# The shifted layers of a transformer stack on one Trainium2 core: the value products in rows of 32, and the products of a tile ordered by array shape

## The reference, cut to what matters

```
x' = shift_tokens(x)                      # second half of the features from the token before
q, k, v = split(x' @ Wqkv)                # 16 heads of 64
q, k = rotary(l2norm(q) * qs), rotary(l2norm(k) * ks)
for each window of 32 tokens: keys of the window before and of its own (64), masked
    out = softmax(8 * q k^T) v
x = x + out @ Wo
x = x + (a * gelu(gate)) @ W2 + b2,  a, gate = split(layernorm(shift_tokens(x)) @ W1 + b1)
```

## Time and profile before

| | |
|---|---|
| median of three runs | 4652.31 us (4650.04 to 4658.37) |
| profiled execution, own time | 4656.79 us |
| its span | 4655.0 us |
| TensorE busy (matmul) | 4112.3 us, 88% |
| VectorE busy | 3561.9 us, 77% |
| ScalarE busy | 2988.6 us, 64% |
| GpSimd busy | 2212.4 us, 48% |
| granted TensorE clock, mean | 0.935 |
| the same, 400 to 3700 us | 1.00 |

### The profile page before, as it was taken

One profiled execution on the slowest core, in us unless ns is written; L12 is line 12 of the kernel. 1 busy time (PEld: TensorE's weight loads), 2 busy tenths in 40 slices (PEclk: granted clock), 3 DMA queues, 4 the chain that ended last, 5 costly groups with the idle time before them and its releaser, 6 DMA issues. The chain is left out here.

```text
span 4655.0 us, 112822 instructions
## 1 busy us (share of the span) xinstructions
PE 4112.3 (88%) x40172; PEld 2362.1 (51%) x40175; DVE 3561.9 (77%) x8496; ACT 2988.6 (64%) x5496; POOL 2212.4 (48%) x1392
## 2 busy tenths in 40 slices
PE   8969999999999999999999999999999953747635
PEld 5644555555555555555555555555555532635533
DVE  7878888888888888888888888888888846356441
ACT  3427777777777777777777777777777745645302
POOL 0006665665656656566566656656565500140006
PEclk9989999999999999999999999999999975868557
DMA  1013222322223222232222322223222200000202
GB/s 41 1 54 67 62 58 62 80 59 61 60 60 81 63 59 60 58 82 65 59 59 60 76 65 63 57 64 75 64 60 61 58 17 12 1 1 6 82 9 35
DMA packets 187828, 246.44 MB, mean 53 GB/s; under 512 B 88677, under 2 KB 129383, under 8 KB 187367
## 3 DMA queue, kind: packets, MB, share of 16 engines
q1 hardware_dynamic: 182054, 240.47, 22.2%
q0 software_dynamic: 5632, 4.33, 0.7%
HBM read 41.65 MB, written 14.30 MB: 12 GB/s over the span
## 5 line engine op out<-in xcount | busy, mean ns | idle before, releaser
L1234 POOL TENSOR_TENSOR f_rot_a<-f_rot_a,f_norm 128x1024 f32<-128x1024 f32 x384 | 730.4, 1902 | 996.1 <-DVE f_norm L1073 963.6
L1226 POOL TENSOR_TENSOR f_rot_a<-f_rot_a,f_rot_b 128x1024 f32<-128x1024 f32 x384 | 908.5, 2366 | 246.3 <-issue 213.6
L832 PE MATMUL f_bank<-f_w_vo,f_xs_t 128*64 128x512 f32 x3072 | 828.5, 617 | 24.5 <-ACT f_vo L1303 24.5
L1303 ACT ACTIVATE f_vo<-f_bank 128x512 f32<-128x512 f32 x768 | 457.0, 595 | 395.9 <-PE f_bank L832 385.9
L1294 ACT ACTIVATE f_squares<-f_bank 128x512 f32<-128x512 f32 x768 | 456.4, 594 | 295.5 <-PE f_bank L819 215.6
L1052 DVE TENSOR_TENSOR f_rot_a<-f_bank,f_rot 128x512 f32<-128x512 f32 x768 | 525.0, 684 | 83.4 <-DVE f_stat L1101 42.3
L1055 DVE TENSOR_TENSOR f_rot_b<-f_bank,f_rot 128x512 f32<-128x512 f32 x768 | 516.8, 673 | 0.0
L864 PEld LDWEIGHTS f_bank<-f_k_t,f_q_t 128*32 128x32 f32 x12288 | 313.6, 109 | 315.4 <-issue 162.4
L1059 DVE TENSOR_REDUCE f_sums<-f_squares 128x16 f32<-128x1024 f32 x384 | 464.9, 1211 | 1.6
L1315 ACT ACTIVATE f_k_t<-f_bank 64x512 f32<-64x512 f32 x768 | 449.2, 585 | 4.8 <-PE f_bank L854 0.3
L1240 POOL TENSOR_TENSOR f_prob<-f_score,f_stat 128x512 f32<-128x512 f32 x384 | 400.4, 1043 | 98.6 <-DVE f_stat L1105 98.6
(11 more groups left out here) (445 smaller groups left out, 7235.4 us busy)
## 6 DMA issues: line engine op xcount, KB each, us to landing
f_vo_off<-f_vo SPq DMA_DIRECT2D x1152, 128.0 KB, 2.3
f_vo_off<-f_vo SPq DMA_DIRECT2D x384, 64.0 KB, 2.0
f_w_qk<-in_Wqk SPq DMA_DIRECT2D x12, 512.0 KB, 5.9
f_vo_dram<-f_vo_pair SPq DMA_DIRECT2D x48, 128.0 KB, 1.8
f_x_shifted<-s_all SPq DMA_DIRECT2D x48, 128.0 KB
f_x_shifted<-s_all SPq DMA_DIRECT2D x48, 127.0 KB
f_w_vo<-f_vo_dram SPq DMA_DIRECT2D x10, 512.0 KB, 4.0
e_w<-in_e_W SPq DMA_DIRECT2D x2, 2048.0 KB, 12.1
```

Source lines behind the costliest of these rows:

```text
L832: done = nc.tensor.matmul(bank[V][64 * n:64 * n + 64, :], x, w_vo[:, 4 * g:4 * g + 4, n, :], start=True, stop=True)
L1226: nc.gpsimd.tensor_tensor(rot_a[:, slot, :, :], rot_a[:, slot, :, :], rot_b[:, g, :, :], ALU.add).then_inc(rot_summed, 1)
L1234: nc.gpsimd.tensor_tensor(heads, heads, over(norm[:, 16 * g:16 * g + 16], [128, 16, HEAD_DIM]), ALU.mult).then_inc(qk_normed, 1)
L1303: nc.scalar.activation(vo[:, g, 2 * (t % 2) + j, :], flat(V), ACT.Copy).then_inc((va_copied, vb_copied)[j], 1)
```

## The change

`values` makes four products with 32 tokens each in place of two with 64, to the same places of bank V. TensorE's order becomes

```diff
@@ values
                 x = chunk_x(t)[:, 64 * j:64 * j + 64]
-                for n in range(2):
-                    done = nc.tensor.matmul(bank[V][64 * n:64 * n + 64, :], x, w_vo[:, 4 * g:4 * g + 4, n, :], start=True, stop=True)
+                for w in range(4):
+                    at = 32 * (w % 2)
+                    done = nc.tensor.matmul(bank[V][32 * w:32 * w + 32, :], x[:, at:at + 32], w_vo[:, 4 * g:4 * g + 4, w // 2, :], start=True, stop=True)
@@ TensorE, body
                     if on(r - 1):
-                        values_a(p, r - 1, 1)
                         turn_q(p, r - 1, 0)
...
                         turn_k(p, r - 1, 0)
-                        values_b(p, r - 1, 1)
...
                     if on(r - 1):
                         scores(p, r - 1, 0)
+                        values_a(p, r - 1, 1)
+                    if on(r - 2):
+                        mix(p, r - 2, 0)
+                    if on(r - 1):
+                        values_b(p, r - 1, 1)
+
                         turn_q(p, r - 1, 1)
...
-                    if on(r - 2):
-                        mix(p, r - 2, 0)
+
                     if on(r):
                         values_a(p, r, 0)
+                    if on(r - 2):
+                        mix(p, r - 2, 1)
                     if on(r - 1):
                         scores(p, r - 1, 1)
                     if on(r):
                         values_b(p, r, 0)
-                    if on(r - 2):
-                        mix(p, r - 2, 1)
@@ VectorE, body
                     if on(r):
                         rotate(p, r, 0, 1, 0)
-                    if r < 3 and on(r - 2):
-                        invert(1)
-                    if on(r):
                         rotate(p, r, 0, 1, 1)
-                    if r == 3 and on(r - 2):
+                    if on(r - 2):
                         total(p, r - 2, 1)
                         invert(1)
...
                         length(p, r, 0)
-                        rotate(p, r, 1, 1, 0)
                     if on(r - 1):
                         highest(p, r - 1, 0)
+                    if on(r):
+                        rotate(p, r, 1, 1, 0)
...
                         rotate(p, r, 1, 1, 1)
+                    if on(r - 1):
+                        total(p, r - 1, 0)
+                        invert(0)
                     if on(r):
                         length(p, r, 1)
                         inverse_lengths(p, r)
-                    if on(r - 1):
-                        total(p, r - 1, 0)
-                        invert(0)
...
-                    if on(r - 1):
-                        highest(p, r - 1, 1)
                     if on(r):
                         rotate(p, r, 1, 0, 0)
                         rotate(p, r, 1, 0, 1)
+                    if on(r - 1):
+                        highest(p, r - 1, 1)
...
-                    if r != 2 and on(r - 1):
-                        total(p, r - 1, 1)
@@ GpSimd, body
                         add_up(p, r, 0)
-                        scale(p, r, 0)
                     if on(r - 1):
                         weigh(p, r - 1, 0)
                     if on(r):
+                        scale(p, r, 0)
                         add_up(p, r, 1)
@@ ScalarE, body
-                    if r < 3 and on(r - 2):
+                    if on(r - 2):
                         exponential(p, r - 2, 1)
                     if on(r - 1):
-                        copy_values(p, r - 1, 1, 0)
                         copy_q(p, r - 1, 0)
-                    if r == 3 and on(r - 2):
-                        exponential(p, r - 2, 1)
...
                         seed(p, r - 1, 0)
-                        copy_values(p, r - 1, 1, 1)
...
                     if on(r - 1):
+                        copy_values(p, r - 1, 1, 0)
+                        exponential(p, r - 1, 0)
+                        seed(p, r - 1, 1)
+                        copy_values(p, r - 1, 1, 1)
                         copy_q(p, r - 1, 1)
                     if on(r):
                         square(p, r, 1, 0)
-                    if on(r - 1):
-                        exponential(p, r - 1, 0)
-                        copy_k(p, r - 1, 1)
-                        seed(p, r - 1, 1)
                     if on(r - 2):
                         copy_prob(p, r - 2, 1)
+                    if on(r - 1):
+                        copy_k(p, r - 1, 1)
```

## The result

The changed kernel takes 5032.8 us (median of four runs, 5029.14 to 5036.96). The kernel before, on the same chip, takes 4653.63 us (four runs, 4650.04 to 4658.37). The ratio is 1.0814, with an interval of 1.0796 to 1.0833: slower by 379 us, where the forecast was slower by 122 us and its range ended at 4860.

The account below looks back on a forecast made before the run. TensorE, nearly gapless, was taken as the bound. A pass of 73.15 us against 70.73 gave +113 us over 47 passes, layer boundaries +13, less some 3 and 4.5: 4775 us, range 4640 to 4860.

Parts of the forecast that it names:

- Costed at nothing: Work moved on GpSimd, VectorE and ScalarE (weigh, scale, invert, total, highest) was expected to add no time.
- The gain step: TensorE: 12 shape changes a round become 4, four 32-column tiles stream like two of 64; 4.4 us a pass saved.
- K1 to S0 is 1.99: Round 3 on TensorE: time from K1 to S0, taken from the kernel before less its wait of 0.59 us.
- some 2.5: Round 3: TensorE waits some 2.5 us before K1, behind VectorE's late statistics and rotation.
- The sum: One pass, the four S0-to-S0 legs 17.9, 16.9, 21.5 and 16.85 us: 73.15 us against 70.73, +2.4.
- The shape gain: TensorE: an S, V or M behind another of its shape costs 0.87 us instead of 1.01.
- The lost cover: Head of each round: without VA1 and VB1, S0 waits for its seed, 3.37 us after Q0; 0.3 to 1.1 us lost.
- The decisive step: Round 2 to 3: shifted x lands 17.4 us after S0, VectorE idles about 5.5; S0 to S0 21.5 us, before 18.03.
- The waits at VB1: VB1 follows VA1 with only M0 between and waits for VA1's copy: +0.1 us.
- The layer boundary: Last pass of a layer: next q and k weights are issued late, K0 waits 2.7 us at five boundaries, 13 us.
- Shape costs stay: Rival: S, V or M behind another kind still costs 1.01 us, 3.4 us a pass; about 4935 us, chance 0.10.
- ScalarE alone: Rival: the landing is no later than ScalarE's chain in round 3; pass 70.7 us, about 4655 us, chance 0.14.

Follow-up runs that it names:

- after_sp: The changed kernel with SyncE's three DMAs of the shifted x moved ahead of what waits for VB1's copy: 4895.96 us, ratio 1.0518.
- order_only: The changed kernel with the value products back in two of 64 columns, the new order kept: 4969.6 us, ratio 1.0676.
- rows32_only: The kernel before with only the value products changed, to four of 32 columns, in the old order: 4797.14 us, ratio 1.0306.
- order_sp: The changed kernel with values in two of 64 columns and the three shifted-x DMAs ahead of what waits for VB1's copy: 4786.2 us, ratio 1.0282.
- padded versions: rows32_only with 64, 128 or 192 empty TensorE instructions once ahead of the loop: 4803.84, 4796.95 and 4796.6 us.
- block32: The kernel before with values in rows of 32 for group 0 alone, 1657 instructions in the body: 4845.13 us, ratio 1.0391.
- trim_block32: The kernel before with rows of 32 for group 0 alone and 28 covered TensorE waits removed, 1629 instructions: 4856.23 us, ratio 1.0423.

## Why the prediction was wrong

**The step that failed: "Costed at nothing".** It lists the moved work of GpSimd, VectorE and ScalarE, and passes over that the change adds instructions to TensorE's own stream. Per pass there are 16 V (four tiles, two groups, two halves) with two products more each: 32 products of four instructions, 128, and one wait. The gain step says that four tiles of 32 columns stream in the time of two of 64, and they do; they take twice the instructions. I worked from busy time alone. The forecast held no term for the fetch; in the pass shown it costs 2.96 us of idle at K0 and, behind it, K0 and the up product with 1.84 and 1.61 us instead of 0.96 and 0.86: 1.6. That is 4.6 us, the larger part of what was missing; the mean of 44 turns is 2.84 and 1.24, 4.1 us. The page of the profile had the row for it, q8.

The Trainium skill (Runtime: NRT & Kernel Launch, Instruction fetch mechanics) describes a mechanism of this kind: TensorE has 128 KiB for instructions, 2048 of them, refilled in blocks of 256; a taken branch to a page outside the current window of two pages must fetch it before execution goes on; crossing a block costs little that shows. These runs agree on the packets of 16 KB and on a fetch at the loop's turn that isn't hidden. They agree with neither size: 2048 would hold the 1722, and two pages, 512, would not hold the 1593 of before, which was not fetched again. The limit here lies between 1597 and 1629.

**A term that was mis-sized: "K1 to S0 is 1.99".** K1 came 19.55 us after S0 of round 2, as forecast (19.5). TensorE stood for 4.93 us ahead of it, 2.85 before TK0 for ScalarE's copy and 2.08 before K1; the forecast wrote "some 2.5", though its own times leave about 5 between the end of the work and K1. Left out was what such a stand does to the clock: K1 and the up product behind it took 1.84 and 1.64 us, and K1 to S0 is 3.48. That is 1.5 us a pass, and S0 to S0 came to 23.0 instead of 21.5. All terms of the forecast were priced at the clock of before, 1.00; the two stretches show 0.93.

**The sum.** 73.15 and 2.96 (idle), 1.6 (clock behind it) and 1.5 (clock behind TK0's and K1's waits) are 79.2 us, against the 78.62 measured. The 0.6 left over lies in legs that came out a little shorter than forecast. Without the fetch a pass would be about 74.0 us and the kernel 4830 to 4850 (an estimate, 5032.8 less 4.6 or 4.1 us in each of 44 turns), just inside the stated range.

**Right, by its own steps.** The shape gain: 0.87 us for a V behind an S. The lost cover: S0 3.37 us behind Q0. The decisive step: the landing 17.34 us after S0, VectorE idle 5.62, K1 waiting; taking it away in after_sp gives 2.9 us a pass, where the forecast put 2.3 between the DMA and ScalarE, before the clock. ScalarE is next, as stated: with the DMA out of the way the seed ends at 19.14 us, where the forecast had 19.1 to 19.2. The leg is 20.35 all the same, by TK0's wait for ScalarE's copy of q, which the forecast did not have, and the clock behind it. The waits at VB1, forecast at 0.1 us, are in the list only twice.

**The layer boundary.** 2.7 us at each of five was too much. In order_only, whose list shows this wait, it is 6.3 us in all:

```profile
PE f_bank L819 <- DMA f_w_qk<-in_Wqk: 6.3, 5, 1.5
```

In the changed kernel it isn't in the list. The gap ahead of K0 is 4.54 us at the boundary at 941 us, and 2.84 and 2.49 in the turns beside it; whether the weights or the fetch make it longer was not taken apart (rows32_only, which issues the weights earlier, also has 5.05 at its boundary at 2079).

**The rivals.** "Shape costs stay" (4935) was nearest in time and wrong in cause: the four tiles run side by side, and the rows show 0.87. "ScalarE alone" (a pass of 70.7, about 4655) can be read in after_sp, where the landing no longer holds round 3: its mean turn of 75.8 less the fetch, 4.3 us there, is 71.5, an estimate, so the rival's sum was near for that case, and its condition did not hold in the changed kernel. None of the rivals had the fetch, so the range could not hold it.

## What to carry to other kernels

Count the instructions that a change adds to a loop body, not only its busy time, and read the instruction queue's line of the profile's page (here 59 packets before): where a body just fits, a few products more can cost a refetch at every turn, 239 us here for 32 instructions (eight products). Price a new stand of TensorE not only with its own length: behind those of 2.4 to 3.5 us here the products ran at 1.2 GHz, in 21 of 44 turns (order_sp) to nearly all (the changed kernel). A reordering that moves a copy later should be followed onto every queue that waits for that copy; moving the DMAs ahead gave back 137 us of the 379.

## What the runs showed of the hardware

- TensorE's loop body stays loaded at 1597 instructions and is fetched again at 1629. At 1721 it is fetched again at each of four places in the program (no padding, 64, 128 and 192: the same 457 packets). Past the limit about 9 packets of 16 KB are fetched in each turn, whatever the excess: 455 and 456 packets in all at 1629 and 1657, and 457 at 1721 and 1722. So it isn't only the part over the limit that is fetched.
- TensorE stands at such a fetch for 2.8 us on average in the changed kernel, 3.4 to 3.5 in rows32_only, its padded versions and block32, and 4.2 in trim_block32, with idle ended by "issue". The next two or three products then run at 1.2 GHz in many turns, not in all: in 28 of 44 in rows32_only.
- A product of 512 columns behind another shape costs 1.01 us, behind its own 0.86 to 0.87, also for four tiles of 32 side by side.
